# The first attention of a two-layer decoder kernel: its loop over heads written out, its causal mask added by VectorE in the instruction that finds the maximum, its exponentials taken in place

## The chip, the cores and the metric

The kernel runs as one program on one core of a Trainium2 chip. The metric is the device time of one execution in microseconds (us). Engines are called by the profile's names: PE is TensorE (PEld its weight loads), DVE is VectorE, ACT is ScalarE, POOL is GpSimd, SP is SyncE, which issues most DMAs.

## What is computed

A decoder of two layers over an input x of 4 batches, 256 tokens and 256 features. Each layer is an attention, a second mixing step and a mixture of experts, each added to its input and normalised. The change is in the first layer's attention alone:

```python
q = split_heads(x @ Wq)          # 16 heads of 128
k = split_heads(x @ Wk)
v = split_heads(x @ Wv)
q = _apply_rope(q, cos, sin)
k = _apply_rope(k, cos, sin)
scores = jnp.einsum('bhqd,bhkd->bhqk', q, k) * scale
causal = jnp.triu(jnp.ones((s, s), dtype=bool), k=1)
scores = jnp.where(causal[None, None], NEG_INF, scores)
attn = jax.nn.softmax(scores, axis=-1)
ctx = jnp.einsum('bhqk,bhkd->bhqd', attn, v)
...
x = _layernorm(x + _L0_attn_ref(...), axis=-1)
```

The second layer's attention has other projections and the same softmax.

## The kernel before

`layer0_attention` writes one instruction stream by hand for each engine; what one engine needs of another it waits for on a semaphore. The work is cut into 64 units, numbered n = 4h + b: head h (0 to 15) and batch b (0 to 3). A unit has 256 query rows in two tiles of 128. Because of the causal mask the first tile meets 128 keys and the second 256, so a unit's scores are 128 x (128 + 256) cells (`CAUSAL`, 384 columns) in one of two PSUM buffers (`a0_score_ps`).

A unit goes through these steps. PE: `scores`, a bf16 matmul that writes the mask into the two diagonal blocks (identity times `mask_bf`, line 238) and then the two float32 products added on top (lines 240 and 241; the trace shows each of those as two matmuls). DVE: `maxima`, two reductions (lines 266 and 267). ACT: `exps`, two exponentials from PSUM into `probs` in SBUF, a ring of four (lines 274 and 276), each followed by the read of its accumulated row sum. DVE: `divide`, a reciprocal (281) and two multiplications (283, 284). PE: `turn`, three transposes (249), two units later. ACT: `keep_turned` (290). PE: `mix`, the products with v (258, 259), three units later. ACT: `keep_mixed_act` (297), four units later.

Beside the units of head h the projections of head h + 1 are made, in six chunks: q and k for the first half of the tokens and v (chunks 0, 1, 2), and the same for the second half (3, 4, 5). `BESIDE` says where: chunks 0 and 1 in unit b = 0, 2 and 3 in b = 1, 4 and 5 in b = 2, none in b = 3. A q or k chunk is six float32r matmuls (lines 72 to 74), then on DVE `rotate_in` (line 459, a product with the cosines, and line 463, a shuffle), then on POOL `rotate` (506 and 510). A v chunk is eight float32 products (407) and a copy by ACT (`keep_v`, 536). The weights' low parts for head h + 2 are cut by ACT (542) and POOL (515).

So in a head the order on PE is, for each b: `scores` of the unit; its chunks; `turn` of the unit two back; `mix` of the unit three back. The order on DVE is: `maxima`; `rotate_in` of its q and k chunks; `divide` of the unit before. In particular DVE has, between chunk 3 and the `turn` of unit b = 1: rotate chunk 3, divide b = 0, maxima b = 2, rotate chunk 4, divide b = 1.

`heads` writes out heads 0 and 1, runs heads 2 to 13 as a hardware loop of six rounds on every engine (`eng.Fori`, two heads a round, semaphore values and addresses in registers), and writes out heads 14 and 15. The second attention (`layer1_attention`) has no such loop, and it already uses `MaskedAttend`: lines 310 and 311 for the scores, 318 for mask and maximum, 324 and 326 for the exponentials.

Of the kernel before, what the change touches and what calls it, by code (L numbers as in the profile page):

```python
# [8 lines left out]
P = 128  # L9
B, S, D = 4, 256, 256  # L10
# [196 lines left out]
class Attend:  # L207
# [84 lines left out]
    def mixed_out(self, b, head):  # L292
        return self.k.ctxT[:, bass.ds(head, 1), b * S:(b + 1) * S].rearrange("p a s -> p (a s)")

# [35 lines left out]
def layer0_attention(nc, k, I):  # L330

    with ExitStack() as stack:
# [10 lines left out]
        proj_ps = m.ps("a0_proj_ps", [P, 2, 512])  # L343
        at = Attend(m, k, "a0", k.y)
        squared = m.sem("a0_squared")
# [17 lines left out]

        def heads(eng, emit):

            emit(0, 0, 0, True, False, True)
            emit(1, 0, 1, False, False, True)
            with eng.Fori(1, H // 2 - 1) as pair:
                emit(2 * pair, pair, 0, False, False, True)
                emit(2 * pair + 1, pair, 1, False, False, True)  # L370
            emit(H - 2, H // 2 - 1, 0, False, False, False)
            emit(H - 1, H // 2 - 1, 1, False, True, False)

        with nc.Block() as block:
            @block.sync
            def _(sp):
                def load(h, par):
                    at_least(sp, v_proj, 2 * (h - 2) + 2)
                    for n, name in enumerate(("L0_attn_Wq", "L0_attn_Wk", "L0_attn_Wv")):
                        sp.dma_start(w[:, par, n], I[name][:, bass.ds(h * HD, HD)].rearrange("(c p) d -> p c d", p=P)  # L380
                                     ).then_inc(w_in[par], 16)
                load(0, 0)
                load(1, 1)
                load_rest(sp, k, I)
                with sp.Fori(1, H // 2) as pair:
                    load(2 * pair, 0)
                    load(2 * pair + 1, 1)

            @block.tensor
            def _(pe):  # L390
                def project(h, pair, par, c):
# [3 lines left out]
                    else:  # L395
                        pe.wait_ge(w_low, 2 * h + PIECE[what] + 1)
                    if isinstance(h, int) and h == 0:
                        pe.wait_ge(x_low, DC * (half + 1))
# [28 lines left out]
                def emit(h, pair, par, first, last, ahead):  # L427
                    for b in range(B):
# [12 lines left out]
                        elif not first:  # L441
                            mix(h - 1, 1 - par, B + b - at.MIX)
                heads(pe, emit)
                at.turn(pe, B * H - 2, B - 2)
# [6 lines left out]
            def _(dve):  # L451
# [33 lines left out]
                def emit(h, pair, par, first, last, ahead):  # L485
                    for b in range(B):
# [6 lines left out]
                        if b or not first:  # L493
                            at.divide(dve, n - 1, (b - 1) % B)
                heads(dve, emit)
                at.divide(dve, B * H - 1, B - 1)

            @block.gpsimd
            def _(pool):
# [23 lines left out]
                def emit(h, pair, par, first, last, ahead):  # L523
                    if ahead:
                        cut_low(h + 2, par)
                    if not last:
                        for c in NQK:
                            rotate(h + 1, c, 1 - par)
                heads(pool, emit)

            @block.scalar
            def _(act):
# [28 lines left out]
                def emit(h, pair, par, first, last, ahead):  # L561
                    for b in range(B):
                        n = 4 * h + b
                        at.exps(act, n, b)
                        if b == 0 and ahead:
                            cut_high(h + 2, pair + 1, par)
                        if b >= at.TURN or not first:
                            at.keep_turned(act, n - at.TURN, (b - at.TURN) % B)
                        if not first:
                            at.keep_mixed_act(act, n - at.KEEP, b, h - 1)  # L570
                        if not last:
                            for c in BESIDE[b]:
                                if c in NV:

                                    at_least(act, at.mixed, 4 * h - 2 + 2 * CHUNKS[c][1])
                                    keep_v(h + 1, 1 - par, c)
                heads(act, emit)
                at.keep_turned(act, B * H - 2, B - 2)
# [2491 lines left out]
```

## Time and profile before

| | us |
|---|---|
| three timed runs, median (lowest to highest) | 1166.76 (1165.85 to 1167.91) |
| the profiled execution, its own time | 1168.87 |
| its span, first to last instruction | 1167.0 |
| mean granted TensorE clock | 0.943 of full |
| busy over the span: PE, DVE, ACT, POOL | 1039.9, 727.1, 572.3, 473.7 |

The first attention lies between about 10 and 287 us of the span; its 64 units' scores begin at 22.9 us and the last at 280.3 us. The profiled execution took 2.1 us more than the median of the timed runs, and 1.9 us of its time lies around the span. A timeline row gives the start, the length, the engine, the source line and the operation, the output and inputs by name, and how often; in brackets stands how long the engine was idle before it and what released it. A row's length holds the pipeline's fill and drain, so two rows in a row overlap: what an instruction costs its engine is the distance from its start to the next start.

### The profile page before, as it was taken

To read this page: it belongs to the slowest core of one execution; us is meant where nothing else is said; L and a number is where in the kernel's file an instruction comes from. 1 tells how busy PE (TensorE), PEld (TensorE's weight loads), DVE (VectorE), ACT (ScalarE), POOL (GpSimd) and SP (SyncE) were. 2 spreads that over 40 slices of the span, in tenths; PEclk is the share of its full clock that TensorE was granted. 3 is DMA by queue.
4 is the path that set the end of the run, shared out by engine and by line. 5 is a ranking of instruction groups with operands and counts; after the bars stand their busy time and mean duration, and the time that the engine had idled before them with its cause. 6 is when DMAs were issued, how large, how long until landed. Compare 5 with 4: busy or idle time off the path is not lost. (4 is left out here: it accounts for less than half of the span.)

```text
span 1167.0 us, 19506 instructions
## 1 busy us (share of the span) xinstructions
PE 1039.9 (89%) x6044; PEld 831.4 (71%) x6044; DVE 727.1 (62%) x2008; ACT 572.3 (49%) x1568; POOL 473.7 (41%) x506
## 2 busy tenths in 40 slices
PE   4999999998993799759899999988978889999993
PEld 3888888887882599627778888845444557778773
DVE  5878777785475366546655662125697557777775
ACT  2354544555222255426566772036784455556542
POOL 5777677763367444366111110010136224433322
PEclk9999999999996799969899999988998989999997
DMA  9600000000001599624202101001003011231001
GB/s 313 256 28 28 27 20 20 27 14 1 1 32 57 168 347 334 224 82 141 88 23 64 29 15 37 1 21 49 2 2 110 1 55 54 64 99 55 1 1 37
DMA packets 83483, 85.43 MB, mean 73 GB/s; under 512 B 8545, under 2 KB 75943, under 8 KB 83280
## 3 DMA queue, kind: packets, MB, share of 16 engines
q1 hardware_dynamic: 76944, 67.00, 18.1%
q10 hardware_dynamic: 3392, 10.16, 2.3%
q0 software_dynamic: 3072, 7.34, 2.1%
q8 instruction: 38, 0.62, 0.2%
q14 instruction: 37, 0.30, 0.1%
HBM read 63.36 MB, written 22.02 MB: 73 GB/s over the span
## 5 line engine op out<-in xcount | busy, mean ns | idle before, releaser
L510 POOL TENSOR_TENSOR a_qk<-h,a_by_sin 128x512 f32<-128x512 f32 x64 | 88.8, 1388 | 5.0
L290 ACT ACTIVATE a_probsT<-a_turn_ps 128x384 f32<-128x384 f32 x128 | 61.8, 483 | 43.7 <-PE a_turn_ps L249 43.7
L318 DVE CUSTOM_DVE_ANT_0 h<-a_score_ps,mask_bf 128x128 f32<-128x128 f32 (+1 forms) x128 | 40.8, 356 | 63.5 <-PE a_score_ps L311 62.9
L72 PE MATMUL a_proj_ps<-a_x_l,a_w_h 128*128 128x512 f32 x128 | 57.5, 449 | 17.0 <-POOL a_w_l L515 16.6
L1231 POOL TENSOR_TENSOR a_w_l<-a_w,a_w_h 128x256 fp32r<-128x256 f32 x30 | 21.9, 731 | 114.5 <-ACT a_w_h L1424 114.3
L274 ACT ACTIVATE y_moe<-a_score_ps,a_nmax 128x128 f32<-128x128 f32 x64 | 23.6, 369 | 87.6 <-DVE a_nmax L267 87.6
L407 PEld LDWEIGHTS a_proj_ps<-a_w,xT 128*128 128x128 f32 x512 | 62.5, 193 | 2.8 <-issue 0.6
L407 PE MATMUL a_proj_ps<-a_w,xT 128*128 128x128 f32 x512 | 62.7, 276 | 0.2 <-DVE hT L463 0.2
L970 POOL TENSOR_TENSOR e_w_l<-e_w,e_w_h 128x512 fp32r<-128x512 f32 x32 | 40.9, 1279 | 52.0 <-ACT e_w_h L1038 52.0
L695 PE MATMUL t_y_ps<-wo,attnT 128*128 128x256 f32 x256 | 57.1, 380 | 0.0
L2477 POOL TENSOR_TENSOR m_up_l<-m_up_w,m_up_h 128x1024 fp32r<-128x1024 f32 x8 | 19.4, 2430 | 92.7 <-ACT m_up_h L2449 92.7
L1471 PE MATMUL p_y_ps<-wo,attnT 128*128 128x256 f32 x256 | 55.5, 379 | 0.8 <-PEq L1203 0.8
L283 DVE TENSOR_SCALAR y_moe<-y_moe,a_rtotal 128x128 f32<-128x128 f32 x64 | 52.7, 824 | 2.3
L1471 PEld LDWEIGHTS p_y_ps<-wo,attnT 128*128 128x128 f32 x256 | 48.6, 190 | 7.5 <-issue 0.9
L695 PEld LDWEIGHTS t_y_ps<-wo,attnT 128*128 128x128 f32 x256 | 47.9, 190 | 6.1
L74 PE MATMUL a_proj_ps<-a_x_h,a_w_l 128*128 128x512 f32 x128 | 51.9, 406 | 0.0
L73 PE MATMUL a_proj_ps<-a_x_h,a_w_h 128*128 128x512 f32 x128 | 51.7, 404 | 0.0
L324 ACT ACTIVATE h<-h,a_nmax 128x128 f32<-128x128 f32 x64 | 25.8, 404 | 49.0 <-DVE a_nmax L318 46.2
L459 DVE TENSOR_TENSOR h<-a_proj_ps,cos_q 128x512 f32<-128x512 f32 x32 | 22.1, 691 | 43.9 <-PE a_proj_ps L74 43.9
L463 DVE STREAM_SHUFFLE hT<-a_proj_ps 128x512 f32<-128x512 f32 x64 | 47.1, 735 | 0.0
L506 POOL TENSOR_TENSOR a_by_sin<-hT,sin_q 128x512 f32<-128x512 f32 x32 | 41.0, 1280 | 13.6 <-DVE hT L463 13.6
L506 POOL TENSOR_TENSOR a_by_sin<-hT,sin_k 128x512 f32<-128x512 f32 x32 | 41.5, 1296 | 9.6 <-DVE hT L463 9.6
(435 smaller groups left out, 3401.7 us busy)
## 6 DMA issues: line engine op xcount, KB each, us to landing
slots<-zeros ACTq DMA_DIRECT2D x4, 2048.0 KB, 16.5
e_rows<-slots SPq DMA_DIRECT2D x32, 256.0 KB, 4.6
e_w<-in_L_ffn_w_dram SPq DMA_DIRECT2D x32, 256.0 KB, 4.7
out_slots<-e_out SPq DMA_DIRECT2D x32, 256.0 KB, 4.1
e_w<-in_L_ffn_w_dram SPq DMA_DIRECT2D x32, 128.0 KB, 4.2
a_w<-in_L_attn_w_q_dram SPq DMA_DIRECT2D x32, 128.0 KB
m_up_w<-in_up_dram SPq DMA_DIRECT2D x8, 512.0 KB, 4.0
a_w<-in_L_attn_Wq_dram SPq DMA_DIRECT2D x16, 128.0 KB, 2.2
```

Source lines behind the costliest of these rows:

```text
L72: pe.matmul(out, left[0], right[1], start=start, stop=False)
L73: pe.matmul(out, left[0], right[0], start=False, stop=False)
L74: return pe.matmul(out, left[1], right[0], start=False, stop=stop)
L283: dve.tensor_scalar(self.probs[:, b, 0:P], self.probs[:, b, 0:P], self.rtotal[:, b, 0:1], None, ALU.mult)
L290: act.activation(self.probsT[:, b % 2, :], self.turn_ps[:, b % 2, 0:CAUSAL], ACT.Copy).then_inc(self.turned_kept, 1)
L407: last = pe.matmul(proj_ps[:, c % 2, t * HD:(t + 1) * HD], k.xT[:, kc, half * HALF + t * P:half * HALF + (t + 1) * P], w[:, par, 2, kc, :] ...
L463: dve.stream_shuffle(swapped[:, r, :], proj_ps[:, c % 2, :], [i ^ 1 for i in range(32)]).then_inc(rot_in, 1)
L506: pool.tensor_tensor(by_sin[:, r2, :].rearrange("p (b s) -> p b s", b=2), swapped[:, r, :].rearrange("p (b s) -> p b s", b=2), sin[:, None ...
L510: pool.tensor_tensor(qk[:, par, 0 if what == "q" else 1, half * HALF:(half + 1) * HALF], by_cos[:, r, :], by_sin[:, r2, :], ALU.add).then_ ...
L695: last = pe.matmul(y_ps[:, t % 2, 0:D], k.ctxT[:, h, t * P:(t + 1) * P], k.wo[:, h, :], start=h == 0, stop=h == H - 1)
L970: pool.tensor_tensor(w13_p.l[:, r], w13[:, r], w13_p.h[:, r], ALU.subtract).then_inc(w_low, 1)
L1471: last = pe.matmul(y_ps[:, t % 2, 0:D], k.ctxT[:, h, t * P:(t + 1) * P], k.wo[:, h, :], start=h == 0, stop=h == H - 1)
```

## The change

Three edits. The attention object is a `MaskedAttend`, so the mask matmul goes, DVE adds the mask in a `tensor_tensor_reduce` that negates, writes the sum to `probs` and leaves the negated maximum, and ACT takes the exponential from `probs` into `probs` with scale -1. The hardware loops on PE, DVE, POOL, ACT and SP are written out for all 16 heads, with constants for registers. Two waits move: `scores` now waits for the maxima of two units back instead of their exponentials, and the wait for the transposes of four units back stands before DVE's maxima instead of before ACT's exponentials.

```diff
@@ -290,7 +290,7 @@
     def mixed_out(self, b, head):
-        return self.k.ctxT[:, bass.ds(head, 1), b * S:(b + 1) * S].rearrange("p a s -> p (a s)")
+        return self.k.ctxT[:, head, b * S:(b + 1) * S]
@@ -341,7 +341,7 @@
-        at = Attend(m, k, "a0", k.y)
+        at = MaskedAttend(m, k, "a0", k.y)
@@ -361,15 +361,10 @@
-        def heads(eng, emit):
-
-            emit(0, 0, 0, True, False, True)
-            emit(1, 0, 1, False, False, True)
-            with eng.Fori(1, H // 2 - 1) as pair:
-                emit(2 * pair, pair, 0, False, False, True)
-                emit(2 * pair + 1, pair, 1, False, False, True)
-            emit(H - 2, H // 2 - 1, 0, False, False, False)
-            emit(H - 1, H // 2 - 1, 1, False, True, False)
+        def heads(emit):
+
+            for h in range(H):
+                emit(h, h // 2, h % 2, h == 0, h == H - 1, h + 2 < H)
@@ -377,14 +372,13 @@
-                        sp.dma_start(w[:, par, n], I[name][:, bass.ds(h * HD, HD)].rearrange("(c p) d -> p c d", p=P)
+                        sp.dma_start(w[:, par, n], I[name][:, h * HD:(h + 1) * HD].rearrange("(c p) d -> p c d", p=P)
-                with sp.Fori(1, H // 2) as pair:
-                    load(2 * pair, 0)
-                    load(2 * pair + 1, 1)
+                for h in range(2, H):
+                    load(h, h % 2)
@@ -440,7 +434,7 @@
-                heads(pe, emit)
+                heads(emit)
```

The class that the attention now uses, which stands in both kernels:

```python
class MaskedAttend(Attend):
    def scores(self, pe, n, b, q, key):
        r = b % 2
        at_least(pe, self.maxed, n - 1)
        pe.matmul(self.score_ps[:, r, 0:P], q(0, P), key(0, P), start=True, stop=True)
        pe.matmul(self.score_ps[:, r, P:P + S], q(P, S), key(0, S), start=True, stop=True).then_inc(self.scored, 1)

    def maxima(self, dve, n, b):
        r = b % 2
        at_least(dve, self.turned, n - self.PROBS + 1)
        dve.wait_ge(self.scored, n + 1)
        for i, cells in enumerate((slice(0, P), slice(P, P + S))):
            done = dve.tensor_tensor_reduce(self.probs[:, b, cells], self.score_ps[:, r, cells], self.k.mask_bf[:, cells],
                                            -1.0, 3e38, ALU.add, ALU.min, self.nmax[:, b, i:i + 1])
        done.then_inc(self.maxed, 1)

    def exps(self, act, n, b):
        act.wait_ge(self.maxed, n + 1)
        act.activation(self.probs[:, b, 0:P], self.probs[:, b, 0:P], ACT.Exp, bias=self.nmax[:, b, 0:1], scale=-1.0,
                       accum_out=self.total[:, b, 0:1])
        act.activation(self.probs[:, b, P:P + S], self.probs[:, b, P:P + S], ACT.Exp, bias=self.nmax[:, b, 1:2],
                       scale=-1.0, accum_out=self.total[:, b, 1:2]).then_inc(self.exped, 1)
```

DVE's queue of the kernel before, in head 1, from the division of unit b = 0 to that of unit b = 1 (`y_moe` is the ring `probs`, `h` and `hT` take the rotation's two products, `a_nmax` the negated maxima):

```order
L281 RECIPROCAL a_rtotal<-a_total 128x2
L283 TENSOR_SCALAR y_moe<-y_moe,a_rtotal 128x128
L284 TENSOR_SCALAR y_moe<-y_moe,a_rtotal 128x256
L266 TENSOR_REDUCE a_nmax<-a_score_ps 128x1
L267 TENSOR_REDUCE a_nmax<-a_score_ps 128x1
L459 TENSOR_TENSOR h<-a_proj_ps,cos_k 128x512
L463 STREAM_SHUFFLE hT<-a_proj_ps 128x512
L281 RECIPROCAL a_rtotal<-a_total 128x2
L283 TENSOR_SCALAR y_moe<-y_moe,a_rtotal 128x128
L284 TENSOR_SCALAR y_moe<-y_moe,a_rtotal 128x256
```

The same place on DVE in the changed kernel, where the rotation's lines are 453 and 457:

```order
L281 RECIPROCAL a_rtotal<-a_total 128x2
L283 TENSOR_SCALAR y_moe<-y_moe,a_rtotal 128x128
L284 TENSOR_SCALAR y_moe<-y_moe,a_rtotal 128x256
L318 ISA y_moe,a_nmax<-a_score_ps,mask_bf 128x128
L318 ISA a_nmax 128x1
L318 ISA y_moe,a_nmax<-a_score_ps,mask_bf 128x256
L318 ISA a_nmax 128x1
L453 TENSOR_TENSOR h<-a_proj_ps,cos_k 128x512
L457 STREAM_SHUFFLE hT<-a_proj_ps 128x512
L281 RECIPROCAL a_rtotal<-a_total 128x2
L283 TENSOR_SCALAR y_moe<-y_moe,a_rtotal 128x128
L284 TENSOR_SCALAR y_moe<-y_moe,a_rtotal 128x256
```

Nothing changes place: each pair of reductions becomes two masked ones, each with a small read of its accumulator.

PE's queue of the kernel before, from the transposes and the mix of unit b = 1 into the next unit's chunk 2:

```order
L249 MATMUL a_turn_ps<-ident,y_moe 128x128 x3
L258 MATMUL a_mix_ps<-a_probsT,a_v 128x256
L259 MATMUL a_mix_ps<-a_probsT,a_v 128x128
L238 MATMUL a_score_ps<-mask_bf,ident_bf 128x2x128
L240 MATMUL a_score_ps<-a_qk 128x128
L241 MATMUL a_score_ps<-a_qk 128x256
L407 MATMUL a_proj_ps<-a_w,xT 128x128 x8
```

The same place on PE in the changed kernel:

```order
L249 MATMUL a_turn_ps<-ident,y_moe 128x128 x3
L258 MATMUL a_mix_ps<-a_probsT,a_v 128x256
L259 MATMUL a_mix_ps<-a_probsT,a_v 128x128
L310 MATMUL a_score_ps<-a_qk 128x128
L311 MATMUL a_score_ps<-a_qk 128x256
L401 MATMUL a_proj_ps<-a_w,xT 128x128 x8
```

One matmul in each unit is gone, and the rest of the queue stands as it was.

## Rows read from the trace of the kernel before

**Rows 1.** Busy us in one stretch: length, PE, PEld, DVE, ACT, POOL, clock, DMA.
```profile
59.12:257.38 198.26, 198.08 (x1263) 173.33 (x1261) 151.66 (x389) 100.36 (x340) 145.97 (x123) 1.00 0.08 24
```

**Rows 2.** All waits between 60 and 256 us: total us, times, longest.
```profile
PEld a_proj_ps L72 <- issue: 4.6, 12, 0.4
PEld a_turn_ps L249 <- DVE y_moe L284: 2.2, 11, 0.2
```

**Rows 3.** Timeline of PE from the scores of unit b = 2.
```profile
103.07 0.27 PE L238 MATMUL a_score_ps<-mask_bf,ident_bf 128*128 128x256 bf16 x1
103.18 0.39 PE L240 MATMUL a_score_ps<-a_qk 128*128 128x128 f32 x2
103.41 0.60 PE L241 MATMUL a_score_ps<-a_qk 128*128 128x256 f32 x2
104.02 0.47 PE L72 MATMUL a_proj_ps<-a_x_l,a_w_h 128*128 128x512 f32 x1
```

**Rows 4.** Timeline of ACT beside rows 3.
```profile
103.27 0.60 ACT L536 ACTIVATE a_v<-a_proj_ps 128x512 f32<-128x512 f32 x1
```

**Rows 5.** Timeline of DVE, 102 to 110 us.
```profile
102.38 0.69 DVE L459 TENSOR_TENSOR h<-a_proj_ps,cos_q 128x512 f32<-128x512 f32 x1 [2.11 <-PE a_proj_ps L74]
...
103.81 1.37 DVE L283 TENSOR_SCALAR y_moe<-y_moe,a_rtotal 128x128 f32<-128x128 f32 x1
...
105.36 0.28 DVE L266 TENSOR_REDUCE a_nmax<-a_score_ps 128x1 f32<-128x128 f32 x1
...
105.89 0.68 DVE L459 TENSOR_TENSOR h<-a_proj_ps,cos_k 128x512 f32<-128x512 f32 x1
...
107.30 1.36 DVE L283 TENSOR_SCALAR y_moe<-y_moe,a_rtotal 128x128 f32<-128x128 f32 x1
108.58 0.34 DVE L284 TENSOR_SCALAR y_moe<-y_moe,a_rtotal 128x256 f32<-128x256 f32 x1
...
109.95 0.29 DVE L283 TENSOR_SCALAR y_moe<-y_moe,a_rtotal 128x128 f32<-128x128 f32 x1
```

**Rows 6.** Timeline of all engines around the transposes of unit b = 1.
```profile
108.97 0.31 PEld L249 LDWEIGHTS a_turn_ps<-ident,y_moe 128*128 128x128 f32 x3 [0.20 <-DVE y_moe L284]
```

**Rows 7.** Timeline of all engines in the second attention, where `MaskedAttend` runs.
```profile
639.38 0.73 POOL L1231 TENSOR_TENSOR a_w_l<-a_w,a_w_h 128x256 fp32r<-128x256 f32 x1 [3.93 <-ACT a_w_h L1424]
...
640.35 0.29 DVE L318 CUSTOM_DVE_ANT_0 h<-a_score_ps,mask_bf 128x128 f32<-128x128 f32 x1 [1.38 <-PE a_score_ps L311]
...
640.91 0.16 DVE L281 RECIPROCAL a_rtotal<-a_total 128x2 f32<-128x2 f32 x1
641.03 0.40 ACT L324 ACTIVATE h<-h,a_nmax 128x128 f32<-128x128 f32 x1 [0.86 <-DVE a_nmax L318]
...
641.83 0.19 ACT L326 ACTIVATION_READ_ACCUMULATOR h<-h,a_nmax 128x1 f32 x1
```

**Rows 8.** Timeline of the first attention: an exponential pair, and POOL's two products.
```profile
103.81 1.29 POOL L506 TENSOR_TENSOR a_by_sin<-hT,sin_q 128x512 f32<-128x512 f32 x1 [0.34 <-DVE hT L463]
...
105.17 1.40 POOL L510 TENSOR_TENSOR a_qk<-h,a_by_sin 128x512 f32<-128x512 f32 x1
...
106.01 0.37 ACT L274 ACTIVATE y_moe<-a_score_ps,a_nmax 128x128 f32<-128x128 f32 x1 [2.13 <-DVE a_nmax L267]
...
106.72 0.20 ACT L276 ACTIVATION_READ_ACCUMULATOR y_moe<-a_score_ps,a_nmax 128x1 f32 x1
```

**Rows 9.** Instructions of line 459, 60 to 256 us: duration ns min/median/max.
```profile
L459 DVE TENSOR_TENSOR h<-a_proj_ps,cos_q x24: 691/692/694, 63.3 to 249.7; 128x512 f32<-128x512 f32 x24
```

**Rows 10.** DMA queues, 95 to 250 us (all of them): packets, MB, share.
```profile
q1 hardware_dynamic: 7344, 3.54, 8.0%
```

**Rows 11.** DMA queues, 560 to 700 us, in the second attention: those of instructions.
```profile
q8 instruction: 7, 0.11, 0.3%
q14 instruction: 7, 0.06, 0.2%
```

**Rows 12.** Timeline of PE in the last head.
```profile
279.59 0.67 PE L258 MATMUL a_mix_ps<-a_probsT,a_v 128*128 128x256 f32 x2 [0.33 <-ACT attnT L297]
```

More of the change, by code:

```diff
@@ L396, in project @@
                         pe.wait_ge(w_low, 2 * h + PIECE[what] + 1)
-                    if isinstance(h, int) and h == 0:
+                    if h == 0:
                         pe.wait_ge(x_low, DC * (half + 1))
@@ L494, in emit @@
                             at.divide(dve, n - 1, (b - 1) % B)
-                heads(dve, emit)
+                heads(emit)
                 at.divide(dve, B * H - 1, B - 1)
@@ L528, in emit @@
                             rotate(h + 1, c, 1 - par)
-                heads(pool, emit)
+                heads(emit)
             @block.scalar
@@ L576, in emit @@
                                     keep_v(h + 1, 1 - par, c)
-                heads(act, emit)
+                heads(emit)
                 at.keep_turned(act, B * H - 2, B - 2)
```

## The prediction

> **What bounds the kernel now.** I read the busy time by stretch first. From 59.12 to 257.38 us, the loop and a little on each side, PE is busy for 198.08 of 198.26 us while DVE has 151.66 and ACT 100.36 [rows 1]. One would conclude that PE alone sets the pace and that every nanosecond taken off PE is gained. The list of waits is there to doubt that, since a busy PE can hide waits of its loads. It has two entries on PEld for the twelve heads of that stretch, and they matter more than their size: 12 waits of about 0.4 us before line 72, which the view can't name, and 11 of 0.2 us before the transposes of line 249, for DVE's line 284 [rows 2].
>
> The timeline explains the first. In unit b = 2 PE starts line 241 at 103.41 us, two matmuls that need about 0.22 us each, and line 72 only at 104.02 us [rows 3]: some 0.17 us late at the start, and the first of the six is slow as well. Chunk 4 reuses the PSUM buffer of chunk 2, which ACT copies out from 103.27 to 103.87 us [rows 4]. So PE waits here for ACT, once a head.
>
> The second is the place on which this prediction rests. DVE starts to rotate chunk 3 at 102.38 us, right when PE has made it, and from there on it has no gap until line 284 of unit b = 1, from 108.58 to 108.92 us [rows 5]. PE's load for that unit's transposes starts at 108.97 us, 0.05 us later, released by it [rows 6]. So a head has two parts. In part A, from the end of chunk 3 to the transposes of b = 1, DVE's run and PE's own work end together. In part B, the rest, DVE waits for PE (2.11 us before the rotation at 102.38) [rows 5], and PE sets the pace.
>
> DVE's run is long because POOL is in its way. Line 283 takes 1.37 us and 1.36 us in part A and 0.29 us at 109.95 us [rows 5]; POOL's line 506 begins at 103.81 us too and lasts 1.29 us [rows 8]. DVE's multiplication stands until POOL's is through, twice a head. The Trainium skill (SBUF — State Buffer, section on who interferes with whom) says that DVE's `tensor_scalar` and a GpSimd operation take a shared pair of ports as a lock, and the later one blocks fully; the trace agrees.
>
> **The change, part by part.** All durations are distances between starts.
>
> *The mask matmul.* Line 238 starts at 103.07 and line 240 at 103.18 us [rows 3]: 0.11 us, in 64 units 7.0 us. That is the most that can be had from PE. In part B (the scores of b = 0 and b = 1) it counts: 2 x 0.11 = 0.22 us a head. In part A (b = 2 and b = 3) it only makes PE wait longer: the wait for ACT's copy grows, as that copy hangs on transposes made before the scores, and what is left of the gain is lost at line 249, which waits for DVE.
>
> *The masked maxima.* The old pair runs from 105.36 to 105.89 us, 0.53 us [rows 5]. The new pair is in the second attention from 640.35 to 640.91 us, 0.56 us, with the accumulator reads inside [rows 7]. One pair lies in part A's run (b = 2), so part A becomes 0.03 us longer. The other three lie where DVE waits anyway. I take 0.03 us; the bounds are 0.03 (nothing beside it) and the wait that POOL can impose (below).
>
> *The exponentials.* From the first start to the second accumulator read it is 0.71 us now [rows 8] and 0.80 us in place [rows 7]: 0.09 us more on ACT, half idle [rows 1]. Units b = 0 and b = 1 are divided about 6 us after their exponentials, so there it costs nothing. One thing hangs on it: ACT's cut of the next weights in unit b = 0, then POOL's whole queue up to the rotation of chunk 3, before which POOL is idle for 0.34 us [rows 8]. That margin shrinks by the 0.22 us by which chunk 3 comes earlier and by up to 0.04 us (0.09 for the exponentials + 0.03 for the maxima - 0.11 for the mask, and 0.03 to spare). About 0.1 us is left, so I cost it at nothing. If it is gone, line 506 starts as much later and DVE's blocked line 283 with it.
>
> *The moved waits.* `scores` waits for something earlier than before, and PE doesn't wait there now. `maxima` waits for transposes that PE made two units earlier: nothing.
>
> *The loops.* Between 95 and 250 us the only DMA queue is that of the weights, no instructions are fetched [rows 10], and PE has no wait but the two above [rows 2]. So there is nothing for the written-out form to remove. It adds fetches; the second attention, written out, has 7 packets on each of two instruction queues in 140 us [rows 11]. I cost both at zero.
>
> *The sum.* Heads 1 to 13: -0.22 + 0.03 = -0.19 us each, -2.5 us. Head 0: b = 0 is hidden behind the long wait for the first weights, b = 1 counts, part A adds: -0.1 us. Head 14 has no weights to cut and its pace in part A comes over POOL, DVE and ACT, so again about one mask is gained: -0.1 us. In the last head, with no projections, PE waits for ACT [rows 12]; each round of that chain has one mask (-0.11), one pair of maxima (+0.03) and one of exponentials (+0.09): 0. Together **-2.7 us**. What follows shifts as a whole. The profiled 1168.87 us would become 1166.2, and the median, 2.1 us lower, 1166.76 - 2.7 = **1164.1 us**.
>
> **The rivals.**
>
> *PE gets its whole gain (chance 0.13).* For this DVE's run must become shorter, which needs line 283 to win its race against POOL's line 506: both start at 103.81 us [rows 5, 8]. Then the run is 1.08 us shorter (1.37 - 0.29) and PE sets the pace in part A too, with only ACT's copy in the way: 3 x 0.11 = 0.33 us a head, 13 x 0.33 + 0.3 = 4.6 us, 1162.1 us; with that copy out of the way as well, all 7.0 us, 1159.8 us. For it: the start times tie, and constants replace registers in both queues. Against it: the race is lost at both places of this head, and heads 1 and 14 are written out with constants already.
>
> *The loops cost something (0.02).* The 12 waits of 0.4 us that the view can't name, 4.6 us, would be the loop's branches and not ACT's copy [rows 2]; then writing out gains them as well: 1164.1 - 4.6 = 1159.5 us. Against it: they are one a head where the loop has one branch for two heads, and ACT's copy ends just before line 72 starts [rows 3, 4]. The Trainium skill (Runtime: NRT & Kernel Launch, section on instruction fetch mechanics) says that a taken branch stalls for a fetch if its target lies outside a small window of pages. These rows show no fetch in the loop [rows 10].
>
> *No difference that can be told (0.32).* A measurement of this kernel tells about 0.2%, 2.3 us, and my own figure is just beyond that. If POOL's margin is not 0.1 but -0.1 us, each head gains 0.1 less: 13 x 0.1 = 1.3 us, and 1165.4 us remain. If part B holds another tie like that of part A, one mask a head is gained or none: -1.1 us or 0.3 us.
>
> *Slower, since POOL blocks the masked maxima (0.07).* In part A the pair starts at 105.36 us, 0.19 us into POOL's line 510, which lasts 1.40 us [rows 5, 8]. If it needs what POOL holds, it waits 1.2 us in each of 14 heads: +16.8 - 2.7 = +14.1 us, 1180.9 us. It decides as soon as a masked maximum waits over 0.2 us a head. Against it: line 459, also one input from PSUM and one from SBUF, takes 691 to 694 ns in all heads, though POOL is at work beside it [rows 9]; and the pair at 640.35 us doesn't test it, as POOL's cut ended at 640.11 us [rows 7]. The same section of the skill says that a DVE instruction with at most one SBUF input, outside the two-port modes, doesn't contend, by which this rival falls.
>
> *Slower, by instruction fetches (0.06).* The written-out queues of five engines must be fetched while the first microseconds' loads run. If each of some seven blocks cost 0.7 us somewhere on PE, that is +4.9 - 2.7 = +2.2 us, 1169.0 us.
>
> **How the numbers follow.** The forecast has 0.40, with 1163.2 to 1165.2 us as its own range (each head's 0.19 between 0.12 and 0.25 us). With most of the first rival's 0.13 and the closest part of the second, which together leave out less than 2 in 10, the range is 1160.5 to 1167.4 us: low enough for most of PE's whole gain, high enough for no gain and some scatter. Faster by over 0.2% (below 1164.4 us) has about two thirds of the forecast's chance, most of the first rival's and a share of the second's edge: 0.48. Within 0.2%: 0.40. Slower: 0.12.
>
> **What the changed profile would show.** From one head's scores to the next it is 0.19 us less than before. PEld's wait at line 249 for line 284 grows from 0.2 to about 0.3 us or more, and PE's own appears. Line 283 still takes 1.36 us twice a head. The masked pair takes 0.56 us from start to start, also beside POOL's line 510. If line 283 is short in part A, the first rival holds; if line 318 is long there, the third; if PE waits at no fixed line, the fourth. The forecast fails if DVE's run is not what releases line 249.

## The result, and the profile after

The changed kernel took 1160.96 us, the median of 20 executions, against 1166.42 us for 20 of the kernel before. One execution of the changed kernel, at 2610.82 us, was disturbed and is left out of the ratio, which is 0.9950 with a 95% interval of 0.9938 to 0.9963. That is 5.8 us less, between 4.3 and 7.2. The forecast was 2.7 us less (1164.1 us). The sign and the range held; the gain is about twice the sum, and the time is below the forecast's own 1163.2 to 1165.2 us.

The profiled execution took 1161.24 us, with a span of 1159.4 us and a mean granted clock of 0.948. The page's part on busy time, for the whole span:

```profile
PE 1028.4 (89%) x5980; PEld 821.8 (71%) x5980; DVE 730.0 (63%) x2136; ACT 575.4 (50%) x1568; POOL 473.8 (41%) x506
```

PE has 64 matmuls fewer than before, one a unit, and DVE 128 instructions more, the accumulator reads. The same stretch as [rows 1], in the same columns, and then all waits of PE and PEld from 60 to 250 us, answering to [rows 2]:

```profile
59.12:257.38 198.26, 196.77 (x1229) 171.42 (x1228) 156.42 (x495) 104.77 (x348) 146.70 (x124) 1.00 0.09 25
```

```profile
PEld a_proj_ps L72 <- issue: 5.9, 12, 0.5
PEld a_turn_ps L249 <- DVE y_moe L284: 2.8, 11, 0.3
```

By the mean of one, the wait at line 72 grew from 0.38 to 0.49 us, as forecast, and that at line 249 from 0.20 to 0.25 us. The forecast also had PE's own wait appear at line 249; the list has none. PE still looks full, with 196.77 of 198.26 us.

DVE's timeline answers to [rows 5]. It is the same place of head 4, from the rotation of chunk 3 to the division of unit b = 1:

```profile
100.65 0.69 DVE L453 TENSOR_TENSOR h<-a_proj_ps,cos_q 128x512 f32<-128x512 f32 x1 [1.86 <-PE a_proj_ps L74]
...
102.09 1.36 DVE L283 TENSOR_SCALAR y_moe<-y_moe,a_rtotal 128x128 f32<-128x128 f32 x1
...
103.63 0.28 DVE L318 CUSTOM_DVE_ANT_0 y_moe<-a_score_ps,mask_bf 128x128 f32<-128x128 f32 x1
...
104.19 0.68 DVE L453 TENSOR_TENSOR h<-a_proj_ps,cos_k 128x512 f32<-128x512 f32 x1
...
105.60 1.36 DVE L283 TENSOR_SCALAR y_moe<-y_moe,a_rtotal 128x128 f32<-128x128 f32 x1
106.89 0.34 DVE L284 TENSOR_SCALAR y_moe<-y_moe,a_rtotal 128x256 f32<-128x256 f32 x1
```

Three of the forecast's signs can be read here. Line 283 is blocked twice, 1.36 us each. The masked pair takes 103.63 to 104.19, 0.56 us from start to start. And it takes that beside POOL's product, which answers to [rows 8]:

```profile
102.08 1.28 POOL L500 TENSOR_TENSOR a_by_sin<-hT,sin_q 128x512 f32<-128x512 f32 x1
103.45 1.40 POOL L504 TENSOR_TENSOR a_qk<-h,a_by_sin 128x512 f32<-128x512 f32 x1
```

What did not come as forecast is the length of a head. I cut each head of heads 3 to 12 as the prediction does: part A from the start of the transposes of b = 3, which follow chunk 3's last product on PE, to those of b = 1; part B is the rest. Medians over the ten heads, each taken by itself, in us, worked out from the start times of line 249:

| | A | B | head |
|---|---|---|---|
| before | 6.92 | 9.46 | 16.37 |
| after | 6.83 | 9.27 | 16.10 |
| change | -0.09 | -0.19 | -0.27 |
| forecast | +0.03 | -0.22 | -0.19 |

In two further traces of each kernel the head is 16.37 us before, and 16.07 and 16.10 us after. The 0.27 us is no scatter. Part B came nearly as written. Part A was to become longer, and became shorter.

PE's timeline shows why, and half of it could be read before the change. PE in the kernel before, at the end of chunk 3 and at the transposes that [rows 6] are about:

```profile
102.09 0.27 PE L249 MATMUL a_turn_ps<-ident,y_moe 128*128 128x128 f32 x1
...
108.58 0.60 PE L241 MATMUL a_score_ps<-a_qk 128*128 128x256 f32 x2
109.02 0.50 PE L249 MATMUL a_turn_ps<-ident,y_moe 128*128 128x128 f32 x3
```

PE in the changed kernel, the same two places:

```profile
100.45 0.49 PE L249 MATMUL a_turn_ps<-ident,y_moe 128*128 128x128 f32 x3
...
106.83 0.60 PE L311 MATMUL a_score_ps<-a_qk 128*128 128x256 f32 x2
107.28 0.55 PE L249 MATMUL a_turn_ps<-ident,y_moe 128*128 128x128 f32 x3
```

First the lower rows. Two score products of 128x256 need 0.44 us when nothing stands behind them (a kernel without any wait, further down, has 105.58 to 106.02). Before, the transposes start 0.44 us after them: PE did not wait. Only its load had, in PE's shadow. The transposes started 0.10 us after the end of DVE's line 284 at 108.92 us [rows 5], where the changed kernel needs 0.05 us (106.89 + 0.34 = 107.23, then 107.28). So DVE had about 0.04 us to spare, and part A was PE's.

Then the upper rows, which are also the end of chunk 3. DVE's rotation started at 102.38 us [rows 5], 0.29 us later; now it starts at 100.65 us, 0.20 us later. The medians over heads 3 to 12 are 0.287 to 0.288 and 0.200 to 0.201 us in three traces of each kernel. DVE has the same rotation there in both; what differs is that its queue is written out. The kernel before holds its own comparison: its heads 1 and 14 are written out, and there the same distance is 0.198 to 0.200 us in all three traces, while in the twelve heads of the loop it is 0.286 to 0.290 us. It is the same in both heads of a round, and a round has one branch; so it is no cost of the branch. This too could be read before the change.

### The profile page after: what moved, and what is told of

It is laid out like the page before. It is cut to its first block and busy times, and to the rows that moved or that the text cites. A ratio compares the mean times of both kernels' runs of the same rounds, so it can differ in the third digit from the quotient of the medians.

```text
span 1159.4 us, 18973 instructions
## 1 busy us (share of the span) xinstructions
PE 1028.4 (89%) x5980; PEld 821.8 (71%) x5980; DVE 730.0 (63%) x2136; ACT 575.4 (50%) x1568; POOL 473.8 (41%) x506
## 5 line engine op out<-in xcount | busy, mean ns | idle before, releaser
L324 ACT ACTIVATE y_moe<-y_moe,a_nmax 128x128 f32<-128x128 f32 x64 | 25.8, 403 | 84.8 <-DVE a_nmax L318 83.9
L318 DVE CUSTOM_DVE_ANT_0 y_moe<-a_score_ps,mask_bf 128x128 f32<-128x128 f32 (+1 forms) x128 | 40.3, 351 | 13.8 <-PE a_score_ps L311 13.8
```

The costliest lines, as they stand in the source:

```text
L318: done = dve.tensor_tensor_reduce(self.probs[:, b, cells], self.score_ps[:, r, cells], self.k.mask_bf[:, cells], -1.0, 3e38, ALU.add, ALU. ...
L324: act.activation(self.probs[:, b, 0:P], self.probs[:, b, 0:P], ACT.Exp, bias=self.nmax[:, b, 0:1], scale=-1.0, accum_out=self.total[:, b, ...
```

## The theory, its rivals and the experiments

**Theory.** Two paths end at the transposes of b = 1, and the later one sets part A. Path P is PE's: it waits for ACT's copy, starts chunk 4 at 1.93 us after the end of chunk 3, and then works without a pause. Its length is the measured 6.92 us before, and 6.92 - 0.11 = 6.81 us without the mask of b = 3 (that of b = 2 is hidden behind the copy). The first of these is the measured value of before and no test. Path D is DVE's: the lag at its start, its run, and 0.055 us to the transposes. From the medians, it is 0.287 + 6.538 + 0.055 = 6.88 us before, and 0.201 + 6.574 + 0.055 = 6.83 us after. The later of the two gives 6.92 and 6.83 us. Both are measured values that went into the sums, since each kernel's later path ends where its part A ends; the tests are e1, e2, e5 and e6. By this neither half of the change gains in part A alone: masked, with all loops kept, path D would be 0.287 + 6.574 + 0.055 = 6.92 us.

**Rivals.** That PE's work alone sets the pace (each product removed or added counts wherever it stands); that the written-out form gains by itself, through the branch; that one path alone, D or the copy, holds part A; and that the gain outside the first attention is real or scatter.

The eight experiments that follow ran in two groups, each beside its own executions of the kernel before (1166.37 and 1165.55 us, medians of 25 and 24).

### e1: masked, written out on DVE alone

```diff
-        at = Attend(m, k, "a0", k.y)
+        at = MaskedAttend(m, k, "a0", k.y)
...
-                heads(dve, emit)
+                for h in range(H):
+                    emit(h, h // 2, h % 2, h == 0, h == H - 1, h + 2 < H)
```

> MaskedAttend as in the changed kernel, and DVE's queue written out; PE, ACT, POOL and SP keep their hardware loops. Theory A (part A of a head, from the end of chunk 3 to the transposes of unit b = 1, is set by two runs that end together, DVE's and that over ACT's copy of chunk 2; in the loop DVE's rotation of chunk 3 starts 0.29 us after PE's last product and in the written-out form 0.20 us, because of DVE's register waits): a head takes 16.10 us as in the changed kernel, and the kernel gains what the change gains, about 5 us. Rival B (the loops of the other engines cost the 0.09 us): 16.19 us a head, 1.2 us less gained. Rival C (the loops cost nothing at all, the whole 0.28 us a head are the mask matmuls): 16.10 us too, and then the next run shows no gain with plain attention either.

Measured: 1161.09 us (8 executions), 0.9955 (0.9937 to 0.9973), and 16.10 us a head. DVE's lag is 0.20 us, as written out everywhere. So the lag belongs to DVE's own queue, and the other four loops leave the length of a head as it is, though not its two parts.

Part A is 6.88 us here, not 6.83. ACT's queue, still a loop, starts the copy 0.08 us later (1.26 us after the end of chunk 3, against 1.18), and now PE itself is named as waiting:

```profile
106.03 0.47 PE L72 MATMUL a_proj_ps<-a_x_l,a_w_h 128*128 128x512 f32 x1 [0.20 <-ACT a_v L537]
```

Path P is then about 6.81 + 0.08 = 6.89 us, and it is the later one. Part B is 0.06 us shorter than in the changed kernel and makes up for it; why, I did not find.

### e2: written out, without the masked maxima

```diff
-        at = MaskedAttend(m, k, "a0", k.y)
+        at = Attend(m, k, "a0", k.y)
```

> All loops written out, but the plain Attend: mask by a matmul, reductions, exponentials from PSUM. Theory A: PE and ACT's copy set the pace in both parts, DVE merely gets 0.1 us more of slack before line 284: 16.33 to 16.38 us a head and no difference to the kernel before (within 1 us). Rival B (loops cost 0.09 us a head by themselves): 16.29 us a head, 1.3 us faster. Rival C: 16.38 us.

Measured: 1165.82 us (12 executions), 0.9991 (0.9977 to 1.0006), and 16.35 us a head, 0.02 less than before. Part A is 6.92 us, unchanged. DVE here:

```profile
102.22 0.69 DVE L453 TENSOR_TENSOR h<-a_proj_ps,cos_q 128x512 f32<-128x512 f32 x1 [2.19 <-PE a_proj_ps L74]
...
107.15 1.35 DVE L283 TENSOR_SCALAR y_moe<-y_moe,a_rtotal 128x128 f32<-128x128 f32 x1
108.42 0.34 DVE L284 TENSOR_SCALAR y_moe<-y_moe,a_rtotal 128x256 f32<-128x256 f32 x1
```

and PE:

```profile
102.02 0.49 PE L249 MATMUL a_turn_ps<-ident,y_moe 128*128 128x128 f32 x3
```

The lag is 0.20 us, so DVE is 0.09 us earlier at line 284, and nobody profits: the transposes start 0.19 us after its end (median). Path P holds them. The rival that the loops themselves cost something on PE falls with this run. Where the ratio's interval includes 1, the head's length does the telling. The rival that the mask matmul alone makes the whole gain expects no gain here too, and this run doesn't part it from the theory. The run that would, the masked maxima with DVE's loop kept, is missing; against that rival stand the measured lag and the sum of path D.

### e3 and e4: two extra products on PE, in b = 2 or in b = 0

Both run the changed kernel with two more of the old mask products in one unit of each head. The scores overwrite them.

```diff
         at_least(pe, self.maxed, n - 1)
+        if b == self.extra_in:
+            diagonals = self.score_ps[:, r, :].rearrange("p (a s) -> p a s", a=2)[:, :, 0:P]
+            for _ in range(2):
+                pe.matmul(diagonals, self.k.ident_bf[:, :],
+                          self.k.mask_bf[:, :].rearrange("p (a s) -> p a s", a=3)[:, ::2, :], start=True, stop=True)
...
         at = MaskedAttend(m, k, "a0", k.y)
+        at.extra_in = 2
```

(`at.extra_in = 0` in e4.)

> The changed kernel with two extra bf16 mask matmuls (2 x 0.11 us) on PE in every unit b = 2, written over by the scores; the result is that of the changed kernel. Theory A: they lie in the wait for ACT's copy of chunk 2 (line 311 to line 72, about 0.28 us late in the changed kernel), so a head stays at 16.10 us. Rival P (PE sets the pace everywhere): 16.32 us a head, 16 x 0.22 = 3.5 us slower than the changed kernel.

> The same two extra matmuls in every unit b = 0 instead. Theory A: part B of a head is PE's own work, so they count in full: 16.32 us a head, 3.3 us slower than the changed kernel. Rival P says the same here; a rival by which POOL's queue sets part B would give 16.10 us.

Measured: e3 1161.00 us (4 executions), 0.9948 (0.9928 to 0.9969), 16.07 us a head. e4 1165.85 us (10 executions), 0.9999 (0.9983 to 1.0016), 16.30 us a head. The same 0.22 us of PE work costs nothing in b = 2 and 0.20 us in b = 0. There the time is back at that of the kernel before, 4.9 us more than the changed kernel's, where the forecast had 3.3. The heads explain 0.20 us each and leave 0.07 us of the gain; in the profile, head 0 took 3.4 us longer as well (25.02 us against 21.67), which one trace can't put down to the edit. PE in e3:

```profile
103.31 0.38 PE L315 MATMUL a_score_ps<-mask_bf,ident_bf 128*128 128x256 bf16 x2
103.53 0.39 PE L317 MATMUL a_score_ps<-a_qk 128*128 128x128 f32 x2
103.75 0.60 PE L318 MATMUL a_score_ps<-a_qk 128*128 128x256 f32 x2
104.25 0.47 PE L72 MATMUL a_proj_ps<-a_x_l,a_w_h 128*128 128x512 f32 x1
```

The products stand at 103.31 us, and line 72 still starts 0.50 us after line 318, where nothing asks for more than 0.44: it waits for the copy, even with two products more. The distance is 0.72 us in the changed kernel (101.66 to 102.38) and 0.61 before [rows 3]: each product only fills the wait. In the list of waits that of PEld at line 72 shrank from 5.9 to 3.4 us. A busy PE, then, has room here for two products a head. The rival "PE alone" needs 0.22 us in both places and falls.

### e5, e6 and e7: take away one path, the other, and both

e5 divides before it rotates, so that path D ends early:

```diff
                         at.maxima(dve, n, b)
+                        if b or not first:
+                            at.divide(dve, n - 1, (b - 1) % B)
                         if not last:
                             for c in BESIDE[b]:
                                 if c in NQK:
                                     rotate_in(h + 1, c)
-                        if b or not first:
-                            at.divide(dve, n - 1, (b - 1) % B)
```

e6 lets ACT copy chunk 2 as soon as PE has made it, ahead of the copies of the transposes and of the mix:

```diff
+                        if b == 1 and not last:
+                            at_least(act, at.mixed, 4 * h - 2)
+                            keep_v(h + 1, 1 - par, 2)
...
-                                if c in NV:
+                                if c in NV and c != 2:
```

e7 has both edits.

> The changed kernel with DVE's queue in another order: the division of the unit before stands ahead of the rotations of a unit, not behind them. Theory A (DVE's run and the way over ACT's copy of chunk 2 end together at the transposes of unit b = 1): DVE's run is out of the way by over 1 us, the way over ACT's copy stays, so part A falls by at most 0.04 us, from 6.83 to about 6.79 us, a head to 16.03 to 16.08 us, and the kernel is within 1 us of the changed one. Rival D (DVE's run alone sets part A): PE's transposes come as soon as its own work is done, 0.3 us earlier, 15.8 us a head, 4.5 us faster than the changed kernel.

> The changed kernel with ACT's copy of chunk 2 ahead of keep_turned and keep_mixed_act in unit b = 1, where it hangs on nothing that PE makes after chunk 2. Theory A: PE no longer waits before chunk 4, and waits as much longer for DVE's line 284 instead: part A stays at 6.83 us, a head at 16.08 to 16.10 us. Rival E (the wait for ACT's copy alone sets part A): 15.8 us a head, 4.5 us faster than the changed kernel.

> Both edits together. Theory A: PE alone sets the pace, part A falls to PE's own work, about 0.3 us less (the 0.28 us wait before chunk 4 and 0.04 us at the transposes), 15.78 to 15.82 us a head and 4.5 us less in all than the changed kernel, 1156.5 us; by rival D or E nothing is gained over the one of the two runs above that gained. Where the first two heads had DVE stand behind POOL, they may gain up to 3 us more.

| | us (executions) | ratio to before | 95% | A | B | head |
|---|---|---|---|---|---|---|
| e5 | 1157.92 (10) | 0.9937 | 0.9915 to 0.9959 | 6.81 | 9.22 | 16.03 |
| e6 | 1159.09 (9) | 0.9941 | 0.9918 to 0.9964 | 6.84 | 9.27 | 16.11 |
| e7 | 1154.69 (6) | 0.9906 | 0.9878 to 0.9934 | 6.44 | 9.24 | 15.67 |

e5 lands on path P (6.81 us), e6 on path D (6.83, measured 6.84), and only both together let go: 0.43 us a head less than the changed kernel. The time of e5 is 3.0 us below the changed kernel's by the medians and 1.5 us by the ratios, where less than 1 us was expected; its heads make 0.9 us of it, most of that in part B. The waits on PE's side in e6, where D is all that is left, from 60 to 250 us:

```profile
PEld a_turn_ps L249 <- DVE y_moe L284: 7.0, 11, 0.6
...
PE a_turn_ps L249 <- DVE y_moe L284: 2.6, 11, 0.2
```

Here PE's own wait stands beside its load's; this is what a bound by DVE looks like. The kernel before had the load's alone. In e7, all waits between 60 and 250 us are these:

```profile
ACT y_moe L324 <- DVE a_nmax L318: 43.1, 37, 1.3
ACT a_probsT L290 <- PE a_turn_ps L249: 41.7, 36, 1.7
DVE y_moe L318 <- PE a_score_ps L311: 39.6, 48, 2.2
POOL a_w_l L509 <- ACT a_w_h L536: 35.8, 12, 3.2
POOL a_by_sin L500 <- DVE hT L457: 5.8, 24, 0.3
```

No row of PE or PEld is left, and the transposes follow the scores at once:

```profile
105.58 0.60 PE L311 MATMUL a_score_ps<-a_qk 128*128 128x256 f32 x2
106.02 0.27 PE L249 MATMUL a_turn_ps<-ident,y_moe 128*128 128x128 f32 x1
```

Moving the division also took most of it out of POOL's way. Line 283 in the changed kernel between 60 and 256 us, duration in ns (min/median/max):

```profile
L283 DVE TENSOR_SCALAR y_moe<-y_moe,a_rtotal x49: 286/745/1367, 60.1 to 253.2; 128x128 f32<-128x128 f32 x49
```

and in e7:

```profile
L283 DVE TENSOR_SCALAR y_moe<-y_moe,a_rtotal x51: 285/289/1017, 60.1 to 254.2; 128x128 f32<-128x128 f32 x51
```

In e7 no line 283 takes 1.36 us any more, though once a head one still takes about 0.97 us. e7 gained 0.11 to 0.15 us a head more than expected, and with 1154.69 us it is the fastest version here: 6.3 us below the changed kernel by the medians, 5.1 us by the two ratios (0.0044 of 1166).

### e8: both edits on the kernel before

> The kernel before, with its loops and its mask matmul, and the same two edits of the order. Theory A: PE alone sets the pace there too: its wait before chunk 4 (0.25 us) goes, 16.12 us a head against 16.38, 4 us faster than before; the difference to e7 is then four mask matmuls a head, 0.44 us on paper, and about 0.33 us, if some of them stay hidden.

Measured: 1159.86 us (12 executions), 0.9951 (0.9927 to 0.9975), 16.09 us a head (A 6.66, B 9.43). Two moves of a few lines, with loops and mask matmul kept, give what the whole change gives. And e8 against e7 prices the change once more, now with PE as the only bound: 16.09 - 15.67 = 0.42 us a head, close to four masks of 0.11 us. I had expected 0.33. The mask's price was right from the start; what decides is how many of the four count. In the kernel as it was, by the sums above, two did by themselves, and a third nearly (0.09 of 0.11 us) once DVE started earlier.

### e9 to e12: before and after again

Two further executions of each of the two kernels, unchanged, for their traces, to see which stage the rest of the gain lies in.

> The kernel before once more, for its trace. The open point is what of the gain lies outside the first attention: its profiled executions differ by 3.9 us at the end of that attention, and by 7.6 us at the end of the span, with 4.6 us of it in the second attention, where the kernel before ran some microseconds at half the clock. Theory S (that part is scatter, which no edit sets): the second attention takes anything from 196 to 200 us here too, and the first ends at 287 us or later, when its first heads have DVE behind POOL. Rival M (the change itself spares it): about 200 us for the kernel before and 196 us for the changed one, each time.

> The changed kernel once more. Theory S: the second attention takes 196 to 200 us, in no relation to that of the kernel before. Rival M: 196 us. A head of the first attention takes 16.10 us in either case, and the attention ends at 283.5 us, or up to 3 us later.

> As for the other repeat of the kernel before: theory S 196 to 200 us in the second attention, rival M 200 us; a head of the first takes 16.38 us.

> As for the other repeat of the changed kernel: theory S 196 to 200 us in the second attention, rival M 196 us; a head of the first takes 16.10 us.

Measured, us, from the traces (the end of the first attention is the first transpose of its output; the second attention runs from its first projection to the first product with its output weights):

| | time | first attention ends | second attention lasts | rest of the span after the first |
|---|---|---|---|---|
| before, first profile | 1168.87 | 287.4 | 200.3 | 879.6 |
| e9, before | 1165.21 | 287.9 | 200.8 | 875.4 |
| e11, before | 1164.97 | 288.0 | 199.1 | 875.1 |
| after, first profile | 1161.24 | 283.5 | 195.7 | 875.9 |
| e10, after | 1160.51 | 284.1 | 198.5 | 874.6 |
| e12, after | 1159.93 | 284.0 | 198.0 | 874.0 |

The first attention ends 3.9 us earlier in the mean, and every trace of the changed kernel is at least 3.3 us ahead of every trace of the one before. That part is shown. Behind it, the second attention, which the change doesn't touch, was shorter in all three traces of the changed kernel, by 2.7 us in the mean. So neither theory came as written: pure scatter is not what these six show, and the changed kernel's 198.5 and 198.0 us are not the 196 us of the other theory. Once the first profile of before is set aside, the whole rest of the span is 875.1 and 875.4 us against 874.0 to 875.9 us, and over the other experiments it lies anywhere between 871.3 (e1) and 877.2 us (e3). Of the 5.8 us measured, 3.9 are the first attention's; where the other 1.9 come from stays open, and the interval (4.3 to 7.2 us) leaves room for most of it to be chance.

All fourteen traces together say a little more. The second attention took 199.1 to 200.8 us in the three traces of before and in e2, and 195.7 to 198.7 us in the ten others. Outside both attentions these two groups don't differ (676.8 and 677.2 us in the mean, with each group spread over 4 to 6 us). So what is gained beyond the first attention lies in the second. It goes with a stop of PE and its clock there, which the last section shows. What ties it to the first attention is not shown: e8, which keeps loops and mask matmul, is among the ten.

## Why the prediction was right or wrong

**The range held partly by luck.** The measured 1160.96 us lies between the two times of the rival "PE gets its whole gain" (1162.1 and 1159.8 us), and what that rival asks for, a short line 283, did not happen. The range reaches so low for that rival's sake and not by the sum. A head's gain of 0.27 us is also outside the forecast's own 0.12 to 0.25 us, and 1.9 us of the gain were in no term.

**The mask matmul in part B: right in place, a little off in size.** Forecast 0.22 us a head, measured 0.19 (0.21 in a second trace). e4 puts 0.20 us back for two such products.

**Part A: wrong, and this is the step that failed.** I wrote that "DVE's run and PE's own work end together" and that what is left of PE's gain "is lost at line 249, which waits for DVE". I had read PEld's wait as the bound. PE's own row at 109.02 us stands 0.44 us behind the one at 108.58, without a wait. DVE was 0.04 us early, not late. The part became 0.09 us shorter and not 0.03 longer: 13 x 0.12 = 1.6 us more than forecast, of which part B took 13 x 0.03 = 0.4 us back.

**The loops at zero: wrong by 0.09 us a head, on one engine.** I argued from fetches and from PE's waits, and found none. Neither is there. The cost was 0.09 us between PE's release and DVE's start, 0.29 us in place of 0.20, which no list of waits shows, since DVE waits there for PE anyway. Heads 1 and 14 of the kernel before had 0.20 us already. By itself it is worth 0.02 us a head (e2). With the mask matmul gone it carries path D from 6.92 to 6.83 us, and so part A's gain; that sum is worked out, no run has the masked maxima in a DVE loop. The Trainium skill (Runtime: NRT & Kernel Launch, section on instruction fetch mechanics) speaks of a stall at a taken branch to a distant target; between 60 and 256 us no run here shows one on PE, looped or not.

**The masked maxima: right.** 0.56 us a pair, also beside POOL's line 504, and DVE's run is 0.04 us longer (forecast 0.03). The rival that POOL blocks them is refuted. By the Trainium skill (SBUF — State Buffer, section on who interferes with whom) a DVE instruction with at most one input from SBUF, outside the two-port modes, has no part in the lock. The masked maximum has one from SBUF and one from PSUM, and the rows agree. So did the race: line 283 lost it twice in every head, and that rival (PE's whole gain) was not needed to explain anything.

**The exponentials and POOL's margin: right.** POOL's line 500 begins at 102.08 us and DVE's line 283 at 102.09, level as before, and 283 takes the same 1.36 us. The 0.09 us on ACT don't show.

**The first and last heads: small terms, off.** From the scores of head 1 to those of head 15 the first profiles differ by 3.8 us (229.4 and 225.6), of which the forecast had 2.6. Head 14 gained 0.15 us (16.56 to 16.41), forecast 0.1. The scores of head 1 begin at 44.28 to 44.51 us before and 44.03 to 44.64 us after, no difference. The last head, forecast at 0, became 0.35 us longer: 13.51 us from its first scores, the mask matmul included, to the end before, 13.86 us after. The chain of PE, DVE and ACT there has every added cost in it and little of the gain; I have not taken it apart. Head 1 of before took 16.35 us in the first profile and 17.15 and 17.17 us in e9 and e11, against 16.01 to 16.04 us in the changed kernel.

**The rest.** The remaining 1.9 us lie outside the first attention. "What follows shifts as a whole" holds within the scatter of the later stages, and not better than that.

**The fetches: right.** From 95 to 250 us the changed kernel has 14 instruction packets where there were none; PE has no wait that belongs to them. The 0.7 us for each of seven blocks in that rival rested on no row, and no run shows such a price.

## What to carry to other kernels

A wait of PEld is no wait of PE. Before an engine is called the bound at some place, look whether the matmul itself starts later than its predecessor allows; a few hundredths of a microsecond of slack decide whether an edit counts. Where two paths meet within 0.1 us, count each of them to the meeting point, before and after, and take the later: here two such sums, made from the two kernels, give part A of e1, e2, e3, e5 and e6 within 0.02 us, and they name the two cheap moves of e7.

## What the hardware showed that I had not expected

**A hardware loop can cost without a fetch.** In the loop, where semaphore values and addresses are in registers, DVE's first instruction after PE's release came 0.29 us after it, in heads 2 to 13 of all four traces with a loop on DVE. With constants it came after 0.20 us: in heads 2 to 13 of the ten other traces, and in the written-out heads 1 and 14 of those four. Whether it is the wait's register or an address's, no run parts. ACT has something like it: its copy in e1 began 0.08 us later than in the written-out kernel, but not in the kernel before, which is also a loop. So it depends on what stands ahead in the queue, and I have no rule for it.

**DVE can lose the race against POOL twice in a row.** DVE in head 0 of e1:

```profile
40.54 1.09 DVE L283 TENSOR_SCALAR y_moe<-y_moe,a_rtotal 128x128 f32<-128x128 f32 x1
41.54 1.37 DVE L284 TENSOR_SCALAR y_moe<-y_moe,a_rtotal 128x256 f32<-128x256 f32 x1
```

POOL in the same microseconds:

```profile
40.25 1.29 POOL L511 TENSOR_TENSOR a_qk<-h,a_by_sin 128x512 f32<-128x512 f32 x1
41.50 1.27 POOL L507 TENSOR_TENSOR a_by_sin<-hT,sin_q 128x512 f32<-128x512 f32 x1
```

Each stands until POOL's current product is over, and POOL's next one comes first. Undisturbed they take 0.29 and 0.35 us. Head 0 took 25.07 us in this trace and 25.02 us in that of e4, but 21.5 to 21.7 us in all six traces of the two kernels. With one trace of e1 and of e4 it stays open whether that is the execution or the edit.

**One late load, and PE's clock with it.** In every trace PE stops for over 2 us at one place of the second attention. PE waits there for a copy by ACT, and ahead of that copy in ACT's queue stands the first use of a weight that comes by DMA. The kernel before:

```profile
563.66 1.22 PE L258 MATMUL a_mix_ps<-a_probsT,v 128*128 128x256 f32 x2 [3.04 <-ACT a_probsT L290]
```

```profile
562.33 0.42 ACT L1424 ACTIVATE a_w_h<-a_w 128x256 fp32r<-128x256 f32 x1 [3.46 <-DMA a_w<-in_L_attn_w_q_dram]
```

Stretches of the kernel before, in the columns of [rows 1]:

```profile
560.00:564.00 4.00, 0.96 (x7) 0.72 (x6) 2.48 (x12) 1.67 (x6) 0.72 (x1) 0.84 0.18 47
564.00:566.00 2.00, 2.00 (x8) 1.73 (x8) 0.00 (x0) 1.89 (x7) 0.02 (x1) 0.50 0.23 66
```

of the changed kernel in its first profile:

```profile
556.00:560.00 4.00, 1.38 (x11) 1.09 (x10) 2.44 (x12) 2.13 (x8) 0.73 (x1) 1.00 0.14 36
560.00:562.00 2.00, 2.00 (x12) 1.65 (x11) 1.04 (x7) 1.83 (x8) 0.40 (x2) 1.00 0.23 66
```

and of the same kernel in e10:

```profile
560.00:562.00 2.00, 2.00 (x9) 1.73 (x8) 0.00 (x0) 1.45 (x6) 0.38 (x2) 0.50 0.23 66
```

After or late in the stop the granted clock was 0.50 of full speed, that is 1.2 GHz, in eleven of the fourteen traces, and the changed kernel is on both sides: PE kept 2.4 GHz in its first profile and fell in e10 and e12. How long it stayed low goes with the two groups above. The granted clock of 2 us stretches makes it about 6.8 us in the three traces of before and in e2, where PE was idle for 3.04 to 3.29 us. It makes it about 3.4 us in e1, e5, e6, e7, e8, e10 and e12 (idle for 2.35 to 2.93 us), and nothing in the first profile of the changed kernel, e3 and e4 (2.62 to 2.89 us). The second attention took 200.1 us in the mean of the first four, 197.5 us in the next seven and 197.2 us in the last three. So the idle time alone doesn't say whether the clock falls, and with or without the short fall the attention took much the same. The 3.4 us more at half the clock are 1.7 us of PE's work at most, an estimate from these lengths, and so they can be a part of the gain outside the first attention. Why the load landed later in those four traces is not shown.
